# A mixture-of-experts layer on one core: packed chunks of rows, and the experts' weights loaded and split for each chunk

## The chip, the cores and the metric

One core of a Trainium2 chip runs the whole layer. The metric is the device time of one execution in microseconds, lower is better.

## What is computed

The input holds 32 x 512 tokens of 256 numbers, all in float32. Cut to what matters:

```python
x = layernorm(x + attention(x))          # 16 heads of 16, 512 keys
logits = x @ Wg.T                        # 8 experts
top_v, top_i = top_k(logits, 2); gates = softmax(top_v)
# each expert takes its first cap = 16384*2*1.25/8 = 5120 rows, the rest are dropped
h = rows_of_expert @ W1[e]               # 256 -> 1024
h = gelu(h[:, :512]) * h[:, 512:]
y = h @ W2[e]                            # 512 -> 256
x = layernorm(x + sum over both experts of gate * y)
```

## The kernel before

The kernel has three stages with a barrier between them. `attention` goes through the 32 sequences and computes attention, the first layer norm and the routing. Its GpSimd queue scatters every token's row (256 numbers and four more: token, gate data, expert) into the DRAM table `expert_rows`, at the next free slot of its expert. The table has 8 x 5120 rows, that is ten chunks of 512 rows per expert, filled with blanks early on. `experts` works through all 80 chunks of this table, expert by expert. `final_norm` computes the last layer norm.

In `experts` a chunk takes this way. SyncE (SP) loads its rows (L1032, four loads of 128 KB, and L1033, the four extra numbers). VectorE (DVE) transposes them (L1178). ScalarE (ACT) rounds them to the matmul's type as a high part (L1129), and VectorE makes the low part, the remainder (L1184). TensorE (PE) multiplies high by high, low by high and high by low, six matmuls of 512 columns for each of eight results (L1091, `hidden`). ScalarE computes gelu (L1133), VectorE the product (L1190), ScalarE its high part (L1139), VectorE its low part (L1195). TensorE makes the output (L1104, `output`), ScalarE scales it by the gate (L1147), and GpSimd (POOL) adds it into DRAM with four indirect adds (L1061). VectorE's `meta` works out gate and token number of the chunk (L1207 to L1211), and SP may load the rows of chunk n+2 only after it. The loops on all engines run in step by semaphores; `output` of chunk n-1 stands between `hidden` 1 and 2 of chunk n.

The weights of an expert are split in high and low parts as well. They are double-buffered by expert: in the second chunk of each expert SP loads the next expert's weights (L175, L176), and GpSimd makes both parts after its adds (L1074, L1076):

```python
for i, (raw, hi, lo) in enumerate(weights.pieces(1 - k.par)):
    pool.tensor_copy(hi, raw).then_inc(s_whi, 1)
    pool.wait_ge(s_whi, k.e * W_PIECES + (i + 1))
    pool.tensor_tensor(lo, raw, hi.bitcast(F32), ALU.subtract).then_inc(s_w, 1)
```

The three pieces are two halves of W1 and the whole of W2, each 128 x 1024 numbers. Most chunks run in hardware loops (`engine.Fori`). The weights of expert 0 are loaded at the end of `attention`, and split there by ScalarE (L660) and VectorE (L920).

## Time and profile before

| | |
|---|---|
| median of 3 runs | 3536.07 us (3529.52 to 3536.82) |
| profiled execution, its own time | 3539.23 us |
| its span | 3537.5 us |
| PE busy | 3328.4 us (94%) |
| DVE busy | 2489.7 us (70%) |
| ACT busy | 2001.0 us (57%) |
| POOL busy | 1156.9 us (33%) |
| mean granted clock of TensorE | 0.968 |

The profile is of one execution. Busy shares are averages over three stages with different limits: `attention` lasts until about 2046 us, `experts` until about 3430 us, `final_norm` until the end. Names such as `out<-ps_out,gate` are the program's tiles, written from read. An engine's idle time is given in brackets with what ended it.

### The profile page before, as it was taken

What the parts mean: (1) busy time and instruction counts of PE and PEld (TensorE: products, weight loads), DVE (VectorE), ACT (ScalarE), POOL (GpSimd) and SP (SyncE); (2) the same over time, 40 slices, a digit from 0 to 9 for tenths busy, and PEclk for the clock granted to TensorE, in tenths of its full rate; (3) what the DMA queues carried; (4) which work ended last, traced back from release to release, by engine and by line L of the source; (5) the groups of instructions that cost most, each with busy time, mean ns of one, the idle gap of its engine ahead of it and who ended that gap; (6) DMA issues with size and microseconds to landing.
All of it is one profiled execution on the core that took longest, in us unless ns stands there. A gap on an engine that the chain in (4) does not pass through costs nothing. (4 is left out here: it accounts for less than half of the span.)

```text
span 3537.5 us, 60085 instructions
## 1 busy us (share of the span) xinstructions
PE 3328.4 (94%) x19714; PEld 2116.9 (60%) x19714; DVE 2489.7 (70%) x5865; ACT 2001.0 (57%) x3877; POOL 1156.9 (33%) x925
## 2 busy tenths in 40 slices
PE   6999999999999999999999779999999999999960
PEld 3444444444444444444444368888888888888850
DVE  5888888888888888888888445545554545554439
ACT  2777777777777777777777434444444444444420
POOL 1013232222313131313222243435343435343334
PEclk7999999999999999999999789999999999999985
DMA  3444555333323232333333244444344434442439
GB/s 98 146 152 153 162 157 166 107 96 86 97 79 101 78 100 79 100 83 88 91 83 93 61 80 63 74 65 69 54 72 61 79 61 63 66 62 45 62 68 339
DMA packets 397856, 339.51 MB, mean 96 GB/s; under 512 B 257720, under 2 KB 315456, under 8 KB 397632
## 3 DMA queue, kind: packets, MB, share of 16 engines
q1 hardware_dynamic: 334656, 252.20, 27.3%
q0 software_dynamic: 58368, 67.74, 11.3%
q10 hardware_dynamic: 4608, 16.78, 1.2%
q8 instruction: 117, 1.92, 0.2%
q14 instruction: 107, 0.88, 0.1%
HBM read 89.92 MB, written 152.17 MB: 68 GB/s over the span
## 5 line engine op out<-in xcount | busy, mean ns | idle before, releaser
L882 DVE TENSOR_REDUCE peak<-ps_rows 128x1 f32<-128x512 f32 x2048 | 1340.2, 679 | 284.1 <-PE ps_rows L557 280.2
L648 ACT ACTIVATE probs<-ps_cols 128x512 f32<-128x512 f32 x2048 | 1118.5, 599 | 266.7 <-PE ps_cols L567 254.8
L1091 PE MATMUL ps_hid<-x_hi,stack 128*128 128x512 f32 x2560 | 805.0, 396 | 32.3 <-DVE x_lo L1184 27.8
L567 PE MATMUL ps_cols<-stack 50*128 50x512 f32 x2048 | 797.9, 460 | 6.0 <-ACT probs L648 5.8
L557 PE MATMUL ps_rows<-stack 48*128 48x512 f32 x2048 | 763.4, 450 | 9.9 <-DMA stack<-qk_lo 7.7
L1061 POOL DMA_INDIRECT x<-out,token x320 | 503.8, 1574 | 800.2 <-ACT out L1147 641.4
L1190 DVE TENSOR_TENSOR hid<-ps_hid,act_in 128x512 f32<-128x512 f32 x320 | 218.9, 688 | 597.6 <-ACT act_in L1133 597.3
L1091 PEld LDWEIGHTS ps_hid<-x_hi,stack 128*128 128x128 f32 x2560 | 476.9, 189 | 142.0 <-DVE x_lo L1184 27.9
L580 PE MATMUL ps_pv<-probs,v 128*17 128x512 f32 x4096 | 541.6, 601 | 1.2 <-ACT probs L648 1.2
L557 PEld LDWEIGHTS ps_rows<-stack 48*128 48x128 f32 x2048 | 314.5, 187 | 372.8 <-DVE peak L882 264.5
L1091 PE MATMUL ps_hid<-x_lo,stack 128*128 128x512 f32 x1280 | 505.8, 395 | 0.0
L422 POOL TENSOR_SCALAR var_eps<-mv 128x4 f32<-128x4 f32 x32 | 7.5, 233 | 1415.1 <-DVE mv L752 1415.1
L1104 PE MATMUL ps_out<-w_buf,h_hi 128*128 128x256 f32 x2560 | 464.8, 283 | 2.9 <-DVE h_lo L1195 2.9
L1104 PEld LDWEIGHTS ps_out<-w_buf,h_hi 128*128 128x128 f32 x2560 | 402.7, 190 | 10.1 <-issue 3.3
L1133 ACT ACTIVATE act_in<-ps_hid 128x512 f32<-128x512 f32 x320 | 190.0, 596 | 309.4 <-PE ps_hid L1091 309.4
L1104 PE MATMUL ps_out<-w_buf,h_lo 128*128 128x256 f32 x1280 | 363.6, 284 | 0.0
L567 PEld LDWEIGHTS ps_cols<-stack 50*128 50x128 f32 x2048 | 322.0, 185 | 60.6 <-ACT probs L648 44.4
L447 POOL DMA_INDIRECT expert_rows<-row,slot x256 | 254.4, 994 | 85.6 <-issue 81.9
L1147 ACT ACTIVATE out<-ps_out,gate 128x256 f32<-128x256 f32 x320 | 125.4, 475 | 273.6 <-PE ps_out L1104 273.6
L1091 PEld LDWEIGHTS ps_hid<-x_lo,stack 128*128 128x128 f32 x1280 | 241.4, 189 | 57.0
L1195 DVE TENSOR_TENSOR h_lo<-hid,h_hi 128x512 fp32r<-128x512 f32 x320 | 237.3, 746 | 15.3 <-ACT h_hi L1139 0.4
L1104 PEld LDWEIGHTS ps_out<-w_buf,h_lo 128*128 128x128 f32 x1280 | 242.4, 189 | 0.0
(131 smaller groups left out, 3603.2 us busy)
## 6 DMA issues: line engine op xcount, KB each, us to landing
stack<-qk_hi SPq DMA_DIRECT2D x1024, 64.0 KB, 2.3
expert_rows<-blank SPq DMA_DIRECT2D x80, 520.0 KB, 3.9
quarters<-expert_rows SPq DMA_DIRECT2D x320, 128.0 KB, 2.7
stack<-qk_lo SPq DMA_DIRECT2D x512, 64.0 KB, 2.3
xs<-in_L_attn_x SPq DMA_DIRECT2D x32, 512.0 KB, 3.7
x<-row SPq DMA_DIRECT2D x32, 512.0 KB
fy<-x SPq DMA_DIRECT2D x32, 512.0 KB, 4.6
out<-fz ACTq DMA_DIRECT2D x32, 512.0 KB, 4.8
```

The source lines that it names most:

```text
L447: pool.indirect_dma_start(table, bass.IndirectOffsetOnAxis(ap=slot[:, c:c + 1], axis=0), row[it.odd][:, t, :], None, bounds_check=table.sh ...
L557: pe.matmul(ps_rows[n % ROWS][:], q_stack[s][part, h, t * P:(t + 1) * P], k_stack[s][part, h, :], start=True, stop=True).then_inc(s_rows, 1)
L567: pe.matmul(ps_cols[j % 2][:], k_stack[g][part, h, t * P:(t + 1) * P], q_stack[g][part, h, :], start=True, stop=True).then_inc(s_cols, 1)
L580: last = pe.matmul(ps_pv[32 * h:32 * h + HD + 1, :], v[par][:, t, HG * g + h, :], probs[:, (HG * t + h) % RING, :], start=t == 0, stop=t = ...
L648: act.activation(probs[:, j % RING, :], ps_cols[j % 2][:], ACT.Exp, scale=SCALE).then_inc(s_exp, 1)
L882: dve.tensor_reduce(peak[s % 2][:, u:u + 1], ps_rows[n % ROWS][:], AX.X, ALU.max, negate=True).then_inc(s_max, 1)
L1061: pool.indirect_dma_start(x1_dram, bass.IndirectOffsetOnAxis(ap=token[buf][:, t:t + 1], axis=0), out[buf][:, t, :], None, bounds_check=n_t ...
L1091: last = pe.matmul(ps_hid[f % 2][:, part, :], w[c.par][k][:, cols], xx[c.odd][:, k, :], start=i == 0, stop=i == 3 * KT - 1)
L1104: last = pe.matmul(ps_out[:, t, :], hh[buf][:, f, t * P:(t + 1) * P], w[par][:, f, :], start=i == 0, stop=i == 3 * FT - 1)
L1133: act.activation(act_in[f % 2][:], ps_hid[f % 2][:, 0, :], ACT.Gelu).then_inc(s_gelu, 1)
L1190: dve.tensor_tensor(hid[f % 2][:], ps_hid[f % 2][:, 1, :], act_in[f % 2][:], ALU.mult).then_inc(s_mul, 1)
L1195: dve.tensor_tensor(h_lo[c.odd][:, f, :], hid[f % 2][:], h_hi[c.odd][:, f, :].bitcast(F32), ALU.subtract).then_inc(s_hlo, 1)
```

## The change

The change makes the number of chunks 72. At the end of `attention` VectorE reads the experts' totals (TensorE adds the counts over the partitions), caps them at 5120, counts each expert's chunks and writes for each of 72 places the chunk of the table and the number of the expert. At most 71 chunks can hold rows, since 64 full chunks hold all rows and each expert but one can add a partly filled one. Places beyond the last used chunk read an extra blank chunk at the table's end.

Since the expert of a place is known only on the chip, the weights are loaded for every chunk, by a number that SP reads from SBUF (`value_load`), into the raw buffers, and split every time: the high parts on ScalarE (`high_w`), the remainders on GpSimd (`low_w`). The two buffers of split weights alternate by chunk. The loop over the chunks is written out in full on every engine. `gate_part` compares with the plan's expert number instead of a counter.

```diff
+    def load_w1(self, engine, e, s_raw1):
         for a in range(QUARTERS):
-            engine.dma_start(self.raw1[a * BLOCK:(a + 1) * BLOCK], self.w1_rows[e, a]).then_inc(s_raw, 16)
-        engine.dma_start(self.raw2, self.w2_rows[e]).then_inc(s_raw, 16)
+            engine.dma_start(self.raw1[a * BLOCK:(a + 1) * BLOCK], self.w1_rows[e, a]).then_inc(s_raw1, 16)
+    def load_w2(self, engine, e, s_raw2):
+        engine.dma_start(self.raw2, self.w2_rows[e]).then_inc(s_raw2, 16)
...
+        self.per = cap // SEQ
+        self.n_chunks = -(-(n_tokens * TOPK // SEQ + EXPERTS - 1) // 2) * 2
+        self.numbers = sb("plan_numbers", [P, 2, self.n_chunks], U32)
+        self.expert = sb("plan_expert", [P, self.n_chunks])
+    def rows(self, engine, n):
+        return engine.value_load(self.numbers[0:1, 0, n:n + 1], min_val=0, max_val=EXPERTS * self.per)
+    def weights(self, engine, n):
+        return engine.value_load(self.numbers[0:1, 1, n:n + 1], min_val=0, max_val=EXPERTS - 1)
...
+            pe.wait_ge(s_pvout, n_seq * GROUPS)
+            pe.wait_ge(s_route, (n_seq - 1) * ROUTE + COUNTED + 3)
+            pe.matmul(ps_pv[:, 0:EXPERTS], ones[:], carry[:], start=True, stop=True).then_inc(s_total, 1)
...
+            numbers = chunk_no[:].rearrange("p (c a) -> p c a", a=1).to_broadcast([P, plan.n_chunks, EXPERTS])
+            dve.wait_ge(s_total, 1)
+            dve.tensor_scalar(total[:], ps_pv[:, 0:EXPERTS], float(cap), None, ALU.min).then_inc(s_plan, 1)
+            dve.wait_ge(s_plan, 3)
+            dve.tensor_scalar(total[:, 0:1], total[:, 0:1], SEQ + 1.0, None, ALU.max).then_inc(s_plan, 1)
+            dve.wait_ge(s_plan, 4)
+            dve.tensor_tensor(reached[:], total[:].rearrange("p (e a) -> p e a", a=1).to_broadcast([P, EXPERTS, per]),
+                              steps[:].rearrange("p (a i) -> p a i", a=1).to_broadcast([P, EXPERTS, per]),
+                              ALU.is_gt).then_inc(s_plan, 1)
+            dve.wait_ge(s_plan, 5)
+            dve.tensor_reduce(own_chunks[:], reached[:], AX.X, ALU.add).then_inc(s_plan, 1)
+            dve.wait_ge(s_plan, 6)
+            for e in range(EXPERTS):
+                dve.tensor_copy(upto[:, e, 0:e + 1], own_chunks[:, 0:e + 1]).then_inc(s_plan, 1)
+            dve.wait_ge(s_plan, 6 + EXPERTS)
+            dve.tensor_reduce(ends[:], upto[:], AX.X, ALU.add).then_inc(s_plan, 1)
+            dve.wait_ge(s_plan, 7 + EXPERTS)
+            dve.tensor_tensor(ended[:], by_chunk(ends), numbers, ALU.is_le).then_inc(s_plan, 1)
+            dve.wait_ge(s_plan, 8 + EXPERTS)
+            dve.tensor_reduce(plan.expert[:], ended[:], AX.X, ALU.add).then_inc(s_plan, 1)
+            dve.tensor_tensor(ended_at[:], ended[:], by_chunk(ends), ALU.mult).then_inc(s_plan, 1)
+            dve.wait_ge(s_plan, 10 + EXPERTS)
+            dve.tensor_scalar(plan.numbers[:, 1], plan.expert[:], float(EXPERTS - 1), None, ALU.min).then_inc(s_plan, 1)
+            dve.tensor_reduce(start[:], ended_at[:], AX.X, ALU.max).then_inc(s_plan, 1)
+            dve.scalar_tensor_tensor(place[:], plan.expert[:], float(per), chunk_no[:], ALU.mult, ALU.add).then_inc(s_plan, 1)
+            dve.wait_ge(s_plan, 13 + EXPERTS)
+            dve.tensor_tensor(place[:], place[:], start[:], ALU.subtract).then_inc(s_plan, 1)
+            dve.wait_ge(s_plan, 14 + EXPERTS)
+            dve.tensor_scalar(plan.numbers[:, 0], place[:], float(EXPERTS * per), None, ALU.min).then_inc(s_plan, 1)
...
+            load_rows(0)
+            load_rows(1)
+            for n in range(n_chunks):
+                if n + 1 < n_chunks:
+                    expert = 0 if n == 0 else plan.weights(sp, n + 1)
+                    wait(sp, s_w, n * W_PIECES - 1)
+                    weights.load_w1(sp, expert, s_raw1)
+                    wait(sp, s_w, n * W_PIECES)
+                    weights.load_w2(sp, expert, s_raw2)
+                if n + 2 < n_chunks:
+                    sp.wait_ge(s_turn, n * KT + KT)
+                    sp.wait_ge(s_meta, n + 1)
+                    load_rows(n + 2)
...
+            def low_w(n, i):
+                raw, hi, lo = weights.pieces(n % 2)[i]
+                pool.wait_ge(s_whi, (n - 1) * W_PIECES + (i + 1))
+                pool.tensor_tensor(lo, raw, hi.bitcast(F32), ALU.subtract).then_inc(s_w, 1)
+            for n in range(n_chunks):
+                if n + 1 < n_chunks:
+                    low_w(n + 1, 0)
+                    low_w(n + 1, 1)
+                if n:
+                    add_out(n - 1)
+                if n + 1 < n_chunks:
+                    low_w(n + 1, 2)
+            add_out(n_chunks - 1)
...
+                wait(pe, s_w, n * W_PIECES - 1)
+                pe.wait_ge(s_xlo, n * KT + KT)
+                hidden(n, 0)
+                hidden(n, 1)
+                if n:
+                    output(n - 1)
+                hidden(n, 2)
+                hidden(n, 3)
...
+            def high_w(n, i):
+                raw, hi, _ = weights.pieces(n % 2)[i]
+                if i == 0:
+                    act.wait_ge(s_raw1, n * W1_LOADED)
+                elif i == 2:
+                    act.wait_ge(s_raw2, n * W2_LOADED)
+                act.copy(hi, raw).then_inc(s_whi, 1)
...
+                more = n + 1 < n_chunks
+                if more:
+                    high_x(n + 1)
+                gelu(n, 0)
+                if more:
+                    high_w(n + 1, 0)
+                gelu(n, 1)
+                high_h(n, 0)
+                if more:
+                    high_w(n + 1, 1)
+                high_h(n, 1)
+                if n:
+                    scale(n - 1)
+                if more:
+                    high_w(n + 1, 2)
+                gelu(n, 2)
+                gelu(n, 3)
+                high_h(n, 2)
+                high_h(n, 3)
```

How the rows of instructions move. First SP, in a chunk late in `experts`; `quarters` and `meta_rows` are the rows of a chunk, `probs` is the raw buffer of the weights, `plan_numbers` the plan. Before, at the last switch of expert:

```order
L1032 DMA quarters<-expert_rows 32x16x64 [waits s_turn,s_meta]
L1032 DMA quarters<-expert_rows 32x16x64 x3
L1033 DMA meta_rows<-expert_rows 128x4x4
L175 DMA probs<-in_L_ffn_W 32x2x1024 [waits s_w]
L175 DMA probs<-in_L_ffn_W 32x2x1024 x3
L176 DMA probs<-in_L_ffn_W 128x4x256
L1032 DMA quarters<-expert_rows 32x16x64 [waits s_turn,s_meta]
```

Now, in every chunk, the loads of rows between the two register reads and those of weights behind them:

```order
L201 TENSOR_LOAD plan_numbers [waits s_meta,s_turn]
L201 ISA x2
L1078 ISA
L1078 DMA quarters<-expert_rows 32x16x64
...
L1079 ISA
L1079 DMA meta_rows<-expert_rows 128x4x4
L204 TENSOR_LOAD plan_numbers
L204 ISA x2
L176 ISA [waits s_w]
L176 DMA probs<-in_L_ffn_W 32x2x1024
...
L179 ISA [waits s_w]
L179 DMA probs<-in_L_ffn_W 128x4x256
```

The pairs of ISA and DMA stand four times for `quarters` and for the first `probs`. Two reads of registers have come in, the five loads of weights now come in every chunk, and the weights of the next chunk wait in the queue behind the rows of the same chunk.

Second GpSimd, before at a switch of expert (`x` is the sum in DRAM, `stack` and `w_buf` the split weights):

```order
L1061 DMA x<-out,token 16384x256 [waits s_scaled,s_add]
L1061 DMA x<-out,token 16384x256 x3
L1074 CAST stack<-probs 128x1024 [waits s_raw,s_out]
L1076 TENSOR_TENSOR stack<-probs,stack 128x1024 [waits s_whi]
L1074 CAST stack<-probs 128x1024
L1076 TENSOR_TENSOR stack<-probs,stack 128x1024 [waits s_whi]
L1074 CAST w_buf<-probs 128x1024
L1076 TENSOR_TENSOR w_buf<-probs,w_buf 128x1024 [waits s_whi]
```

and now in every chunk:

```order
L1110 TENSOR_TENSOR stack<-probs,stack 128x1024 [waits s_whi] x2
L1103 DMA x<-out,token 16384x256 [waits s_add,s_scaled]
L1103 DMA x<-out,token 16384x256 x3
L1110 TENSOR_TENSOR w_buf<-probs,w_buf 128x1024 [waits s_whi]
L1110 TENSOR_TENSOR stack<-probs,stack 128x1024 [waits s_whi] x2
```

The casts have left GpSimd, and two of the three subtractions stand ahead of the adds. The casts are now on ScalarE, in every chunk:

```order
L1168 CAST x_hi<-turned 128x512 [waits s_turn] x2
L1180 ACTIVATE act_in<-ps_hid 128x512 [waits s_hid]
L1176 CAST stack<-probs 128x1024 [waits s_raw1]
L1180 ACTIVATE act_in<-ps_hid 128x512 [waits s_hid]
L1186 CAST h_hi<-hid 128x512 [waits s_mul,s_out]
L1176 CAST stack<-probs 128x1024
L1186 CAST h_hi<-hid 128x512 [waits s_mul]
L1194 ACTIVATE out<-ps_out,gate 128x256 [waits s_add,s_meta,s_out]
L1194 ACTIVATE out<-ps_out,gate 128x256 x3
L1176 CAST w_buf<-probs 128x1024 [waits s_raw2]
L1180 ACTIVATE act_in<-ps_hid 128x512 [waits s_hid] x2
L1186 CAST h_hi<-hid 128x512 [waits s_mul] x2
```

The three casts of weights (L1176) stand between gelus and high parts of h, each in front of instructions that VectorE's products and low parts wait for.

## Rows read from the trace of the kernel before

**Rows 1.** Timeline, GpSimd: start us, us, engine line op, names, count [idle before].
```profile
2082.07 1.58 POOL L1061 DMA_INDIRECT x<-out,token  x1 [39.80 <-ACT out L1147]
...
2234.74 1.55 POOL L1061 DMA_INDIRECT x<-out,token  x1 [9.61 <-ACT out L1147]
...
2240.30 1.67 POOL L1061 DMA_INDIRECT x<-out,token  x1 [0.30 <-issue]
...
2251.62 1.55 POOL L1061 DMA_INDIRECT x<-out,token  x1 [9.65 <-ACT out L1147]
...
3406.42 1.56 POOL L1061 DMA_INDIRECT x<-out,token  x1 [9.59 <-ACT out L1147]
```

**Rows 2.** Waits from 2150 to 3390 us: engine, name, line, releaser: us, times, longest.
```profile
PE ps_hid L1091 <- DVE hid L1190: 4.2, 6, 1.4
```

**Rows 3.** Timeline, ScalarE, a chunk without a switch.
```profile
2243.91 0.61 ACT L1139 CAST h_hi<-hid 128x512 fp32r<-128x512 f32 x1
...
2249.17 1.57 ACT L1147 ACTIVATE out<-ps_out,gate 128x256 f32<-128x256 f32 x4 [3.78 <-PE ps_out L1104]
...
2251.97 0.60 ACT L1133 ACTIVATE act_in<-ps_hid 128x512 f32<-128x512 f32 x1 [1.23 <-PE ps_hid L1091]
```

**Rows 4.** Timeline, VectorE, the same chunk.
```profile
2241.86 1.29 DVE L1184 TENSOR_TENSOR x_lo<-turned,x_hi 128x512 fp32r<-128x512 f32 x2
...
2244.65 1.46 DVE L1195 TENSOR_TENSOR h_lo<-hid,h_hi 128x512 fp32r<-128x512 f32 x2
...
2246.37 0.17 DVE L1211 COPY token<-meta_rows 128x4 uint32<-128x4 uint32 x1
```

**Rows 5.** Timeline, the DMA issues of SyncE, around the first switch shown.
```profile
2233.74 1.72 SPq L175 DMA_DIRECT2D probs<-in_L_ffn_W  x4
...
2235.50 0.43 SPq L176 DMA_DIRECT2D probs<-in_L_ffn_W  x1
...
2246.62 1.91 SPq L1032 DMA_DIRECT2D quarters<-expert_rows  x4
...
2248.57 0.49 SPq L1033 DMA_DIRECT2D meta_rows<-expert_rows  x1
```

**Rows 6.** Landing of the loads of line 175, then 176, 2225 to 2245 us.
```profile
DMA to landing us min/median/max: 3.4/4.5/5.7
...
DMA to landing us min/median/max: 6.5/6.5/6.5
```

**Rows 7.** Timeline, GpSimd and then VectorE, a chunk with a split of weights.
```profile
2260.03 2.73 POOL L1076 TENSOR_TENSOR stack<-probs,stack 128x1024 fp32r<-128x1024 f32 x1
...
2264.29 2.40 POOL L1076 TENSOR_TENSOR stack<-probs,stack 128x1024 fp32r<-128x1024 f32 x1
...
2268.22 2.73 POOL L1076 TENSOR_TENSOR w_buf<-probs,w_buf 128x1024 fp32r<-128x1024 f32 x1
...
2258.78 4.53 DVE L1184 TENSOR_TENSOR x_lo<-turned,x_hi 128x512 fp32r<-128x512 f32 x2
...
2264.95 3.74 DVE L1195 TENSOR_TENSOR h_lo<-hid,h_hi 128x512 fp32r<-128x512 f32 x2 [0.44 <-ACT h_hi L1139]
...
2268.61 2.36 DVE L1207 SCALAR_TENSOR_TENSOR gate_part<-meta_rows,expert_no 128x4 f32<-128x4 f32 x1
```

**Rows 8.** Timeline, ScalarE and VectorE, end of the first stage.
```profile
2028.42 1.04 ACT L660 CAST w_buf<-probs 128x1024 fp32r<-128x1024 f32 x1
...
2032.54 1.22 DVE L920 TENSOR_TENSOR w_buf<-probs,w_buf 128x1024 fp32r<-128x1024 f32 x1
...
2046.79 0.06 DVE L1171 MEMSET expert_no<- 128x1 f32 x1 [13.02 <-PEq L197]
```

**Rows 9.** Busy by stretch: us; PE, PEld, DVE, ACT, POOL; PEclk, DMA share, GB/s.
```profile
1984.00:1988.00 4.00, 3.23 (x22) 0.83 (x14) 0.43 (x3) 3.18 (x7) 0.00 (x0) 1.00 0.00 0
...
2056.00:2060.00 4.00, 4.00 (x11) 3.08 (x10) 1.29 (x2) 1.87 (x3) 0.00 (x0) 0.53 0.00 0
...
2060.00:2064.00 4.00, 4.00 (x19) 3.24 (x18) 1.31 (x3) 1.67 (x3) 0.00 (x0) 1.00 0.01 4
```

More of the change, by code:

```diff
@@ L151 @@
 QUARTERS, BLOCK = P // 32, 32
-LOADED = 16 * (QUARTERS + 1)
+ROWS_LOADED = 16 * (QUARTERS + 1)
+W1_LOADED, W2_LOADED = 16 * QUARTERS, 16
 W_PIECES = 3
@@ L273, in attention @@
         token = sb("token", [P, TILES])
+        total = sb("total", [P, EXPERTS])
+        steps = sb("steps", [P, per])
+        reached = sb("reached", [P, EXPERTS, per])
+        own_chunks = sb("own_chunks", [P, EXPERTS])
+        upto = sb("upto", [P, EXPERTS, EXPERTS])
+        ends = sb("ends", [P, EXPERTS])
+        chunk_no = sb("chunk_no", [P, plan.n_chunks])
+        ended = sb("ended", [P, plan.n_chunks, EXPERTS])
+        ended_at = sb("ended_at", [P, plan.n_chunks, EXPERTS])
+        start = sb("start", [P, plan.n_chunks])
+        place = sb("place", [P, plan.n_chunks])
         s_const = sem("s_const")
@@ L370, in body @@
                         sp.wait_ge(s_pv, n_seq * UNITS)
-                        weights.load(sp, 0, s_raw)
+                        weights.load_w1(sp, 0, s_raw1)
+                        weights.load_w2(sp, 0, s_raw2)
                     if it.filling:
@@ L1107, in output @@
                 last.then_inc(s_out, 1)
-            def body(k):
-                if k.lead and not k.odd:
-                    wait(pe, s_w, k.e * W_PIECES)
-                pe.wait_ge(s_xlo, k.n * KT + KT)
-                hidden(k, 0)
-                hidden(k, 1)
-                if not k.first:
-                    output(1 - k.par if k.lead and not k.odd else k.par, 1 - k.odd, k.n - 1)
-                hidden(k, 2)
-                hidden(k, 3)
-            chunks(pe, body)
-            output(1, (n_chunks - 1) % 2, n_chunks - 1)
+            for n in range(n_chunks):
+                wait(pe, s_w, n * W_PIECES - 1)
[6 more added lines that the diff above has]
+                hidden(n, 3)
@@ L1213, in _ @@
-            turn(0, 0, LOADED)
-            low_x(0, 0)
-            def body(k):
-                if not (k.last and k.odd):
-                    turn(1 - k.odd, k.n + 1, (k.half + (k.odd + 1)) * LOADED)
-                    low_x(1 - k.odd, k.n + 1)
-                product(k, 0)
-                product(k, 1)
-                low_h(k, 0)
-                low_h(k, 1)
-                meta(k)
-                product(k, 2)
-                product(k, 3)
-                low_h(k, 2)
-                low_h(k, 3)
@@ L1230, in _, with meta @@
-            chunks(dve, body)
+            def meta(n):
+                wait(dve, s_scaled, n * TILES - TILES)
+                wait(dve, s_add, n * ADDED - ADDED)
+                r = meta_rows[n % 2]
+                dve.scalar_tensor_tensor(gate_part[:], r[:, :, C_E0 - DIM], plan.expert[:, n:n + 1], r[:, :, C_DIFF - DIM],
+                                         ALU.is_equal, ALU.mult).then_inc(s_gp, 1)
+                dve.wait_ge(s_gp, n + 1)
+                dve.tensor_tensor(gate[n % 2][:], gate_part[:], r[:, :, C_G1 - DIM], ALU.add)
+                dve.tensor_copy(token[n % 2][:], r[:].bitcast(U32)[:, :, C_ID - DIM]).then_inc(s_meta, 1)
@@ L1233, in final_norm @@
+            turn(0)
+            low_x(0)
+            for n in range(n_chunks):
+                if n + 1 < n_chunks:
+                    turn(n + 1)
+                    low_x(n + 1)
+                product(n, 0)
+                product(n, 1)
+                low_h(n, 0)
+                low_h(n, 1)
+                meta(n)
+                product(n, 2)
+                product(n, 3)
+                low_h(n, 2)
+                low_h(n, 3)
 def final_norm(nc, y_dram, out_dram):
```

202 lines of the change are left out of this document (69 added, 133 removed).

## The prediction

> **What bounds the kernel now.** The kernel has three stages, and the change touches the second, so I read that one. The GpSimd adds mark its rhythm: every chunk of 512 rows ends in four indirect adds, and the first of chunk 0 starts at 2082.07 us, the first of chunk 78 at 3406.42 us [rows 1]. That is 1324.35 us for 78 chunks, 16.98 us each. A chunk without a switch of expert takes 16.88 us (2251.62 - 2234.74), [rows 1] as well. The waits of the stage say who sets this: TensorE waited 4.2 us in 1240 us, six times, always for the product on VectorE [rows 2]. So TensorE bounds the stage, and the only disturbance is the seven switches of expert. Every other engine has slack: ScalarE's scaling of a chunk starts at 2249.17 us and its next gelu at 2251.97 us [rows 3], and GpSimd's adds fill only 7.2 us of a chunk (2234.74 to 2241.97 us) [rows 1].
>
> **What is taken away.** 80 chunks become 72. TensorE's work in a chunk is the same, whatever the rows hold. If a chunk kept its length, 8 x 16.98 = 136 us would go.
>
> **What is added to every chunk.** Before, weights were loaded and split seven times in the stage; now 71 times. Five loads are issued on SP, three casts of 128x1024 are made on ScalarE, three subtractions of 128x1024 on GpSimd, and SP reads two numbers from SBUF into registers. I cost each.
>
> *ScalarE* gets 3 x 1.04 us (the same cast at the end of the first stage) [rows 8]. Two stand between gelu 0 and the scaling, where no matmul of the chunk is short of them. The third stands between scaling (ends 2250.74) and gelu (starts 2251.97): 1.23 us of slack takes 1.04. By itself this costs nothing.
>
> *GpSimd* gets 3 x 2.40 to 2.73 us [rows 7]; with 7.2 us of adds and a 0.9 us handover from ScalarE this is about 16 us of a chunk of 16.88. It fits, barely, and is no bound alone.
>
> *VectorE* gets no instruction, but its subtractions are held up. Undisturbed, two low parts of x take 1.29 us and two of the hidden rows 1.46 us [rows 4]. While GpSimd splits weights, the same pairs take 4.53 and 3.74 us, and a gate product of 128x4 takes 2.36 us, ending just when GpSimd's subtraction does (2270.97 against 2270.95) [rows 7]. So a VectorE instruction with two SBUF inputs waits for the whole GpSimd instruction. The products that read PSUM are not held.
>
> *SP and the loads* close a circle, and this is where I think the new bound lies. SP's queue is in order: the rows of chunk n+2 (after meta of chunk n), then the first-layer weights of n+2, then the second-layer ones. ScalarE can cast those weights only when they have landed, GpSimd subtracts only then, VectorE's low parts wait for GpSimd, meta stands behind them, and meta releases the next rows. One turn, from meta to meta:
>
> 1. meta ends at 2246.54 us (2246.37 + 0.17) [rows 4], SP issues at 2246.62 [rows 5]: 0.08.
> 2. Register read for the rows: no row shows one. Below, 0.17, the shortest VectorE copy [rows 4]; above, a whole DMA on this queue, which for these loads is 3.4 us at least [rows 6]. I take 0.75, a DMA issue on SP (0.49) and a handover between engines with it (about 0.25), because it moves one word and no packets. The Trainium skill, DMA: Bandwidth & Descriptors, section "Latency and other measured facts", gives a floor of about 0.6 us for a tensor_load; by that each turn would be 0.3 us shorter than by mine, 21 us over the stage. No trace here shows it.
> 3. Issue of five row loads: 2246.62 to 2249.06: 2.44 [rows 5].
> 4. Second register read: 0.75.
> 5. First-layer weights. The four issues start at 2233.74 and take 1.72 [rows 5]; the latest landed up to 5.7 us after its own issue, so about 1.4 + 5.7 = 7.1 after the first [rows 6]. The second-layer load (0.5 MB, behind it then) will now come later. It landed at 2235.50 + 6.5 = 2242.0, and the 1.5 MB took some 6.2 us, so its share in front of the last quarter was about 0.9. I take 6.2; the bounds are 4.8 (1.4 + the shortest landing, 3.4) and 7.1.
> 6. From landing to meta: handover 0.1, cast 1.04, GpSimd's first subtraction 2.40, one low part on VectorE 0.73, GpSimd's second 2.40, the other low part 0.73, then gate, sum and token 0.43 (2246.54 less 2244.65 less 1.46): 7.8 [rows 4, 7, 8]. If VectorE went first each time, only ScalarE's chain would count: two casts, a gelu, two h casts at 0.6 [rows 3], a low part and 0.43, some 5.1. With 2.73 for both subtractions it is 8.5.
>
> Sum: 0.08 + 0.75 + 2.44 + 0.75 + 6.2 + 7.8 = **18.0 us**. That is longer than 16.88, so TensorE should wait about 1.1 us per chunk, for the product behind meta. The lower bound of the circle (12.7) lies below TensorE's 16.88, which is then the period. The upper (0.08 + 3.4 + 2.44 + 3.4 + 7.1 + 8.5) is 24.9.
>
> *The second-layer weights* have a circle of their own through adds (7.2), the last subtraction (2.7), the load (6.5 at most), cast, gelu, product and TensorE's 11.3 us to the next scaling: about 33 us for two chunks, 16.5 each. No bound, but close.
>
> *The plan* is some 22 small VectorE instructions of about 0.2 us and four of 576 elements (under 1 us each): 8 us at most. VectorE ends its last subtraction at 2033.76 us and idles 13 us to the stage's start at 2046.79, because GpSimd's scatters are still going [rows 8]. Cost nothing; without that cover 8 us. One more blank fill on SP, two counters at the start and the longer straight-line program: nothing, for SP and GpSimd idle there; both signs within 3 us.
>
> **The sum.** Counting 70 steps between first adds of chunk 0 and 70 in place of 78: time = 3539.2 - 1324.4 + 70 x T, with T the new period. The profiled run was 3539.2 us, 3.2 above the median, so against the median I use 3536 - 1324.4 + 70 x T. With T = 18.0: 2211.6 + 1260 = **3472 us**. The change loses its gain at T = 18.92. A measurement here can tell about 0.2%, 7 us, or 0.1 us of T.
>
> **Rivals.**
> *A, the circle does not close.* Loads land early enough, or VectorE's low parts mostly slip in front of GpSimd. T = 16.9, 3394 us. For it: all three lower bounds lie well below mine. Against it: GpSimd would have to lose a race that it won in rows 7. Chance 0.20.
> *Forecast*, T from 17.0 to 18.9, 3402 to 3535 us. Chance 0.50.
> *C, slower: the register reads are dear.* They stand in front of both groups of loads, on the queue that everything waits for. The point from which this decides is 1.2 us each (0.92 more in the turn). At 1.5 us each T = 19.5 and the time is 3577 us; at the price of a whole DMA (3.4) T = 23.3, 3843 us. For it: nothing hides them. Against it: one word is not a DMA. Chance 0.22.
> *D, slower: the clock.* TensorE was granted 1.00 (2.4 GHz) in a stretch where it was busy 3.23 of 4 us, and 0.5 (1.2 GHz) in the idle start of the stage, where 11 matmuls took the time of 19 [rows 9]. If waits of 1 us in each chunk brought the low clock, each chunk would take 16.9 x 19/11 = 29 us: 4242 us if always, about 3680 if a fifth of the chunks. Busy at 94% is well above the 81% at which the row still shows full clock. The Trainium skill, TensorE: Matmul & The Clock Gate, section "HAM oscillation — how this bites in real kernels", warns that pauses between bursts of matmuls bring this on; by it the slow case would be real, by the row it is not. Chance 0.08.
> That the chunks are not fewer is excluded: the loops are written out for 72.
>
> **How the numbers follow.** The point is the likeliest case, 3472. Its own range is 3402 to 3535. The range of 8 in 10 goes down to A (3390) and up to C at 1.5 us (3577), and leaves out dearer reads and D. Faster: A and nearly all of the forecast, 0.70; same 0.05; slower, C and most of D, 0.25.
>
> **What would show it.** Right: chunks 17.5 to 18.5 us apart by the adds; TensorE waiting about 1 us per chunk for the product; ScalarE waiting several us for the weights in front of its first cast; VectorE's low parts of h near 2.4 us each; SP taking 4 us from meta to the first weight load. Step 2 is wrong if the gap in front of the row loads is not near 0.75; step 5 if the weights land in under 5 or over 7 us; step 6 if landing to meta is not 7 to 8.5. The forecast as a whole is wrong if ScalarE does not wait for raw weights, or if the clock in the stage is under 1.00.

## The result, and the profile after

| | before | after |
|---|---|---|
| median of 4 runs | 3532.80 us (3528.88 to 3536.82) | 3596.55 us (3593.22 to 3601.08) |
| profiled execution, its own time | 3539.23 us | 3595.22 us |
| its span | 3537.5 us | 3593.7 us |
| mean granted clock of TensorE | 0.968 | 0.957 |

The change makes the kernel **slower**: the ratio is 1.0185, 95% interval 1.0168 to 1.0202, clear of the noise (on another chip it was 1.0223, below). Forecast was 3472 us, faster, with a range up to 3577.

The page's busy times and two of its 40-slice rows, kernel after:

```profile
PE 3245.0 (90%) x18947; PEld 2014.0 (56%) x18947; DVE 2632.9 (73%) x5758; ACT 2123.3 (59%) x3978; POOL 1608.1 (45%) x1066
...
PEclk7999999999999999999999699999999999999985
DMA  3445454333333333333332366666666666666639
```

From slice 23 on the second stage runs: the DMA engines are busy for six tenths there, where the first stage has three. GpSimd has 450 us more work than before, VectorE 143, ScalarE 122.

The rhythm, GpSimd's timeline, first adds of chunk 0 and of chunk 70 (as [rows 1]):

```profile
2085.36 1.86 POOL L1103 DMA_INDIRECT x<-out,token  x1 [0.16 <-issue]
...
3465.41 1.56 POOL L1103 DMA_INDIRECT x<-out,token  x1 [5.02 <-ACT out L1194]
```

These are 1380.05 us for 70 steps, a period T of 19.71 us instead of 16.98. The part of the time outside these steps is 3595.22 - 1380.05 = 2215.2 us; before it was 3539.23 - 1324.35 = 2214.9. So the whole loss is in T.

Waits of the kernel after, 2200 to 3400 us (as [rows 2]: engine, name, line, releaser: us in total, times, longest):

```profile
ACT x_hi L1168 <- DVE turned L1227: 390.8, 60, 7.8
DVE turned L1227 <- DMA meta_rows<-expert_rows: 301.9, 60, 6.3
POOL stack L1110 <- ACT stack L1176: 250.2, 60, 5.9
DVE hid L1239 <- ACT act_in L1180: 165.2, 63, 4.4
ACT stack L1176 <- DMA probs<-in_L_ffn_W: 141.9, 60, 3.8
PE ps_hid L1132 <- DVE hid L1239: 122.9, 73, 2.7
```

and of SP, the engine that issues the loads:

```profile
SPq L1092 <- DVE token L1256: 593.4, 61, 11.4
```

In each of 60 chunks every engine waits for another one, and the list closes on itself: SP waits for VectorE's token (the end of `meta`), VectorE for the rows that SP loads, ScalarE for the weights that SP loads behind them, GpSimd for ScalarE. TensorE, which before waited 4.2 us in the stage [rows 2], waits 123 us in 1200.

**One turn of the circle**, from the end of one `meta` to the end of the next. VectorE, SP, ScalarE, GpSimd, VectorE from the timelines of 2700 to 2745 us (start us, us, engine, line):

```profile
2718.29 0.16 DVE L1256 COPY token<-meta_rows 128x4 uint32<-128x4 uint32 x1
...
2719.25 2.04 SPq L1078 DMA_DIRECT2D quarters<-expert_rows  x4
2721.48 0.39 SPq L1079 DMA_DIRECT2D meta_rows<-expert_rows  x1
2722.62 1.81 SPq L176 DMA_DIRECT2D probs<-in_L_ffn_W  x4
...
2725.81 1.30 DVE L1227 STREAM_TRANSPOSE turned<-quarters 128x512 f32<-128x512 f32 x2 [4.79 <-DMA meta_rows<-expert_rows]
...
2728.16 0.39 SPq L179 DMA_DIRECT2D probs<-in_L_ffn_W  x1
...
2730.41 1.05 ACT L1176 CAST stack<-probs 128x1024 fp32r<-128x1024 f32 x1 [2.15 <-DMA probs<-in_L_ffn_W]
...
2731.54 5.23 POOL L1110 TENSOR_TENSOR stack<-probs,stack 128x1024 fp32r<-128x1024 f32 x2 [3.54 <-ACT stack L1176]
...
2732.60 4.72 DVE L1244 TENSOR_TENSOR h_lo<-hid,h_hi 128x512 fp32r<-128x512 f32 x2
...
2737.58 0.16 DVE L1256 COPY token<-meta_rows 128x4 uint32<-128x4 uint32 x1
```

Token ends at 2718.45; 0.80 us later the rows are issued, for 2.62 us; after 0.75 us more the first weight load is issued; 7.79 us later ScalarE casts; 7.33 us after that the next token ends (2737.74): 19.29 us. The same five differences, taken over the 68 turns from 2100 to 3440 us in which the trace names the weights' landing as what ScalarE's cast waited for:

| step | forecast | measured, mean |
|---|---|---|
| 1 + 2: meta to first row load | 0.83 | 0.82 |
| 3: issue of five row loads | 2.44 | 2.85 |
| 4: to the first weight load | 0.75 | 0.84 |
| 5: first weight load issued, to ScalarE's cast | 6.3 | 7.95 |
| 6: from the cast's start to meta | 7.7 | 7.32 |
| turn | 18.0 | 19.77 |

(The forecast's handover of 0.1 us between landing and cast stands in row 5 here.)

TensorE in this turn, its timeline and then one-microsecond stretches (us; PE, PEld, DVE, ACT, POOL busy; granted clock, DMA share, GB/s):

```profile
2719.19 1.19 PE L1132 MATMUL ps_hid<-x_hi,stack 128*128 128x512 f32 x2 [2.54 <-DVE hid L1239]
```

```profile
2719.00:2720.00 1.00, 0.81 (x2) 0.75 (x3) 0.91 (x3) 0.93 (x2) 0.69 (x2) 0.50 0.00 0
2720.00:2721.00 1.00, 1.00 (x3) 0.75 (x3) 1.00 (x2) 0.29 (x1) 1.00 (x1) 0.50 1.03 97
...
2724.00:2725.00 1.00, 1.00 (x6) 0.82 (x5) 0.00 (x0) 0.00 (x0) 0.99 (x2) 1.00 1.51 267
...
2730.00:2731.00 1.00, 1.00 (x11) 1.00 (x10) 0.00 (x0) 0.59 (x1) 0.00 (x0) 1.00 0.94 301
2731.00:2732.00 1.00, 1.00 (x10) 1.00 (x10) 0.01 (x1) 1.00 (x3) 0.46 (x1) 1.00 0.52 183
```

TensorE stands still for 2.54 us, then has a granted clock of 0.50 (1.2 GHz) until about 2722 us: the matmul pair of 0.63 us takes 1.19. And the DMA engines are full, or nearly, from 2720 to 2731 us, which covers the whole time in which the circle waits for them. (The profile gives shares over 1 there; I read them as full.)

### The profile page after: what moved, and what is told of

Its sections match the earlier page's. It is cut to its first block and busy times, and to the rows that moved or that the text cites. A ratio compares the mean times of both kernels' runs of the same rounds, so it can differ in the third digit from the quotient of the medians.

```text
span 3593.7 us, 57839 instructions
## 1 busy us (share of the span) xinstructions
PE 3245.0 (90%) x18947; PEld 2014.0 (56%) x18947; DVE 2632.9 (73%) x5758; ACT 2123.3 (59%) x3978; POOL 1608.1 (45%) x1066
## 5 line engine op out<-in xcount | busy, mean ns | idle before, releaser
L1132 PE MATMUL ps_hid<-x_hi,stack 128*128 128x512 f32 x2304 | 768.4, 416 | 170.8 <-DVE hid L1239 143.1
L1132 PEld LDWEIGHTS ps_hid<-x_hi,stack 128*128 128x128 f32 x2304 | 444.3, 199 | 305.2 <-issue 162.1
L1110 POOL TENSOR_TENSOR stack<-probs,stack 128x1024 fp32r<-128x1024 f32 x142 | 370.0, 2631 | 315.6 <-ACT stack L1176 315.6
L1132 PE MATMUL ps_hid<-x_lo,stack 128*128 128x512 f32 x1152 | 473.1, 411 | 0.0
L1244 DVE TENSOR_TENSOR h_lo<-hid,h_hi 128x512 fp32r<-128x512 f32 x288 | 430.8, 1533 | 6.7 <-ACT h_hi L1186 0.7
L1146 PE MATMUL ps_out<-w_buf,h_hi 128*128 128x256 f32 x2304 | 407.0, 280 | 2.9 <-DVE h_lo L1244 2.9
L1168 ACT CAST x_hi<-turned 128x512 fp32r<-128x512 f32 x144 | 87.4, 622 | 479.9 <-DVE turned L1227 479.9
L1146 PEld LDWEIGHTS ps_out<-w_buf,h_hi 128*128 128x128 f32 x2304 | 356.4, 188 | 9.7 <-issue 3.3
L1227 DVE STREAM_TRANSPOSE turned<-quarters 128x512 f32<-128x512 f32 x144 | 94.0, 690 | 364.1 <-DMA meta_rows<-expert_rows 364.1
L1146 PE MATMUL ps_out<-w_buf,h_lo 128*128 128x256 f32 x1152 | 321.9, 279 | 0.0
```

What stands on the lines that cost most here:

```text
L1132: last = pe.matmul(ps_hid[f % 2][:, part, :], w[n % 2][k][:, cols], xx[n % 2][:, k, :], start=i == 0, stop=i == 3 * KT - 1)
L1146: last = pe.matmul(ps_out[:, t, :], hh[n % 2][:, f, t * P:(t + 1) * P], w[n % 2][:, f, :], start=i == 0, stop=i == 3 * FT - 1)
L1244: dve.tensor_tensor(h_lo[n % 2][:, f, :], hid[f % 2][:], h_hi[n % 2][:, f, :].bitcast(F32), ALU.subtract).then_inc(s_hlo, 1)
```

## The experiments

The theory and its rivals. **Circle**: the turn above sets the period; whatever shortens it shortens T by as much, until TensorE's own 16.9 us or the next longest circle. **Volume**: the weight traffic itself (1.5 MB a chunk) is what the stage can't carry. **Lock**: GpSimd's subtractions hold VectorE up, and that alone makes the chunk long. **Clock**: the half-clock phases of TensorE make it long. Ratios are against the kernel before on the same chip. T is the mean distance of the tokens of all chunks in the profiled execution; after has 19.64 by this count, before 16.90. Steps of a turn are given as in the table above.

**e_reads: the two register reads taken out of the turn.** SP reads both numbers before it waits.

```diff
-                    expert = 0 if n == 0 else plan.weights(sp, n + 1)
...
                 if n + 2 < n_chunks:
+                    rows = plan.rows(sp, n + 2)
+                    expert = plan.weights(sp, n + 2)
                     sp.wait_ge(s_turn, n * KT + KT)
                     sp.wait_ge(s_meta, n + 1)
-                    load_rows(n + 2)
+                    load_rows(n + 2, rows)
```

> Both register reads of chunk n+2 are made before SP waits for meta of chunk n, so they leave the circle. Circle theory: a turn of 19.6 us loses 0.74 + 0.84 = 1.6 us, so T = 18.1 and the time is 3597 - 70 x 1.6 = about 3487 us, and the gap from the end of meta to the first row load falls from 0.8 to 0.1 us. Lock theory (VectorE and GpSimd holding each other up set the rhythm by themselves): no change, 3597. Load-volume theory (the DMA engines can't move the 2.5 MB of a chunk faster): no change, 3597.

Measured: 3519.42 us, ratio 0.9961 (0.9945 to 0.9977), T 18.58. The gain is 77 us, two thirds of what the circle had promised; the other two theories expected none. The same place on VectorE and SP, timelines of 2700 to 2740 us:

```profile
2716.68 0.17 DVE L1257 COPY token<-meta_rows 128x4 uint32<-128x4 uint32 x1
...
2717.06 2.08 SPq L1077 DMA_DIRECT2D quarters<-expert_rows  x4
2719.33 0.39 SPq L1078 DMA_DIRECT2D meta_rows<-expert_rows  x1
2719.90 2.16 SPq L176 DMA_DIRECT2D probs<-in_L_ffn_W  x4
```

Over 64 turns the steps are 0.22, 2.75, 0.20, 8.20, 7.35, in sum 18.71. Each read is worth 0.60 and 0.64 us. The Trainium skill, DMA: Bandwidth & Descriptors, section "Latency and other measured facts", gives a floor of some 600 ns for a tensor_load; these two differences agree with it. What the expectation took out, 0.74 and 0.84, held handovers that stayed. The landing of the weights, which now stand closer behind the rows, is 0.25 us longer than in after. Chips differ by nearly as much (r_after, below); e_dvereads has this on one chip and shows that the term is not a constant.

**e_halfw1: half of the first-layer weights loaded.** Columns 0 to 511 of W1 only; this kernel leaves the rest of the weights out.

```diff
-            engine.dma_start(self.raw1[a * BLOCK:(a + 1) * BLOCK], self.w1_rows[e, a]).then_inc(s_raw1, 16)
+            engine.dma_start(self.raw1[a * BLOCK:(a + 1) * BLOCK, :, 0:FF], self.w1_rows[e, a][:, :, 0:FF]).then_inc(s_raw1, 16)
```

> Only half the columns of the first-layer weights are loaded (the other half keeps old values), so part of the computation is left out; instructions and waits are the same. Circle theory: the landing term of 7.95 us falls by about 2.3 us (0.5 MB at 220 GB/s), T = 17.3, time about 3435 us. Load-volume theory: the bytes of a chunk fall by a fifth, T = 15.7, so TensorE's 16.9 sets it, 3405. Lock theory: no change, 3597.

Measured: 3440.21 us, ratio 0.9743 (0.9727 to 0.9759), T 17.45. The landing fell from 7.95 to 5.55 us, the others stayed (0.81, 3.00, 0.95, 7.43), in the 31 turns in which ScalarE still waited for it. In these turns half of a megabyte is worth 2.4 us; T fell by 2.2. Waits, 2200 to 3200 us:

```profile
DVE turned L1227 <- DMA meta_rows<-expert_rows: 235.7, 56, 5.8
ACT stack L1176 <- DMA probs<-in_L_ffn_W: 16.9, 29, 1.6
```

In 57 chunks VectorE waits for its rows 56 times, ScalarE for the weights only 29 times: in the other turns something else closes the circle. There is a second way round from meta to meta, through the rows of the chunk. In the turn of after shown above it takes 0.80 us to the first row load, 6.56 to the transposes (2725.81 us) and 11.93 to the next token, and the last part holds the 2.15 us in which ScalarE waited for the weights. Without that wait it would be some 17.1 us, an estimate from these rows, and T came out at 17.45. Circle and volume both say that T falls, so this run only prices the term; the next run tells them apart.

**e_meta: the circle opened.** SP waits for `meta` only because it would overwrite `meta_rows`. With four buffers it need not; the wait on the transposes stays.

```diff
-        meta_rows = [sb(f"meta_rows{i}", [P, TILES, ROW - DIM]) for i in range(2)]
+        meta_rows = [sb(f"meta_rows{i}", [P, TILES, ROW - DIM]) for i in range(4)]
...
-                sp.dma_start(meta_rows[n % 2][:], chunk_meta[rows]).then_inc(s_rows[n % 2], 16)
+                sp.dma_start(meta_rows[n % 4][:], chunk_meta[rows]).then_inc(s_rows[n % 2], 16)
...
                     sp.wait_ge(s_turn, n * KT + KT)
-                    sp.wait_ge(s_meta, n + 1)
                     load_rows(n + 2)
```

> Four buffers for the extra numbers in place of two, and SP no longer waits for meta before it loads the rows of chunk n+2; the bytes, the splits and the reads stay. Circle theory: the circle is open, the first-layer weights wait only for GpSimd's second subtraction; its own circle is 0.1 + 7 + 6.4 = 14 us, so TensorE's 16.9 sets the period: 3400 to 3425 us. Lock theory: no change, 3597. Load-volume theory: no change, 3597.

Measured: 3403.62 us, ratio 0.9639 (0.9623 to 0.9655), T 16.91. Waits of TensorE for the product, 2150 to 3200 us, and SP's and VectorE's timeline from 2700 us:

```profile
PE ps_hid L1131 <- DVE hid L1238: 4.1, 2, 2.4
```

```profile
2716.59 0.39 SPq L179 DMA_DIRECT2D probs<-in_L_ffn_W  x1
2717.75 2.59 SPq L1078 DMA_DIRECT2D quarters<-expert_rows  x4
...
2721.77 1.81 SPq L176 DMA_DIRECT2D probs<-in_L_ffn_W  x4
...
2722.56 0.16 DVE L1255 COPY token<-meta_rows 128x4 uint32<-128x4 uint32 x1
```

The rows now go out right behind the second-layer weights, 4.8 us ahead of the token that they used to wait for. The same bytes are moved, the same splits made by the same engines, and T is that of the kernel before (16.90). So neither the volume nor the lock was what held T at 19.6; one wait was, for a buffer of 8 KB. It makes the circle a shown cause: all of the 2.7 us per chunk that after had lost against before went with that wait, which stood in front of the rows and so in both ways round. The clock rose again with it, so this run doesn't price the clock; see rival D below. A run with four buffers and the wait kept was not made.

**e_dve: the remainders on VectorE.** The three subtractions of a chunk move from GpSimd to VectorE, between products and low parts; the wait stays.

```diff
                 product(n, 0)
+                low_w(n + 1, 0)
                 product(n, 1)
                 low_h(n, 0)
+                low_w(n + 1, 1)
                 low_h(n, 1)
...
                 product(n, 2)
+                low_w(n + 1, 2)
                 product(n, 3)
```

> VectorE makes the three remainders of the weights (1.22 us each) in place of GpSimd; GpSimd only adds. Circle theory: from cast to meta the turn falls from 7.3 to about 5.8 us, nothing else: T = 18.1, about 3490 us. Lock theory: no lock is left, T = 16.9, 3405 us. Load-volume theory: no change, 3597.

Measured: 3462.63 us, ratio 0.9808 (0.9792 to 0.9825), T 17.84. VectorE's timeline from 2700 us:

```profile
2722.03 1.23 DVE L1253 TENSOR_TENSOR stack<-probs,stack 128x1024 fp32r<-128x1024 f32 x1 [3.10 <-ACT stack L1166]
...
2724.37 1.22 DVE L1253 TENSOR_TENSOR stack<-probs,stack 128x1024 fp32r<-128x1024 f32 x1
2725.51 0.69 DVE L1234 TENSOR_TENSOR h_lo<-hid,h_hi 128x512 fp32r<-128x512 f32 x1
2726.45 0.17 DVE L1246 COPY token<-meta_rows 128x4 uint32<-128x4 uint32 x1
```

A weight's remainder takes 1.22 us instead of 2.4 to 2.7, a low part of h 0.69 instead of 2.4 (4.72 for two above). Step 6 fell from 7.32 to 5.66 us, the turn to 17.98 (66 turns), near the 18.1 that the circle theory said; with the lock as the whole cause it would have been 16.9. So the lock is real, but as a term of the circle, worth 1.66 us.

*The following batch (e_order to e_metadve) ran on a chip whose first stage took about 225 us longer, with and without the change (before: 3758.18 us); only its ratios and its second stage are compared. The changed kernel itself was not run there, so its steps are compared with those of another chip; between two other chips its T differed by 0.22 us (r_after, below).*

**e_order: the weights ahead of the rows.** SP issues the first-layer weights of chunk n+2 before the rows of n+2, hence outside the wait for `meta`.

The old loads of chunk n+1 at this place are gone, and those of chunk 1 stand ahead of the loop.

```diff
...
                 if n + 2 < n_chunks:
+                    expert = plan.weights(sp, n + 2)
+                    sp.wait_ge(s_w, (n + 1) * W_PIECES - 1)
+                    weights.load_w1(sp, expert, s_raw1)
                     sp.wait_ge(s_turn, n * KT + KT)
                     sp.wait_ge(s_meta, n + 1)
                     load_rows(n + 2)
+                    sp.wait_ge(s_w, (n + 1) * W_PIECES)
+                    weights.load_w2(sp, expert, s_raw2)
```

> SP issues the first-layer weights of chunk n+2 ahead of the rows of chunk n+2, as soon as GpSimd's second subtraction is done; the wait for meta stays in front of the rows. Theory that the weights' landing of 7.95 us is long because the rows are just in front of them: landing falls to about 6, and the circle through the weights is open; what is left runs meta, read 0.8, issue 2.8, landing of rows 5, transposes, low parts and products back to meta, 15 to 17.8 us: T = 16.9 to 17.8, 3400 to 3465 us. Theory that the adds alone make it long: landing stays near 8, but T still falls since the circle is shorter.

Measured: 3824.61 us, ratio 1.0182 (1.0163 to 1.0201), T 19.65. My expectation missed: as slow as the changed kernel instead of 2 to 4% under before. SP's and VectorE's timelines of 2900 to 2945 us, and the wait that ends VectorE's longest idle time, 2400 to 3400 us:

```profile
2905.49 1.84 SPq L176 DMA_DIRECT2D probs<-in_L_ffn_W  x4
2908.15 2.02 SPq L1078 DMA_DIRECT2D quarters<-expert_rows  x4
...
2906.11 0.16 DVE L1257 COPY token<-meta_rows 128x4 uint32<-128x4 uint32 x1
2915.96 1.31 DVE L1228 STREAM_TRANSPOSE turned<-quarters 128x512 f32<-128x512 f32 x2 [6.34 <-DMA meta_rows<-expert_rows]
```

```profile
DVE turned L1228 <- DMA meta_rows<-expert_rows: 367.5, 51, 8.7
```

The weights are no longer waited for; the rows are. They stand 0.8 us behind 1 MB of weights, and the transposes start 7.8 us after their first issue (8.06 in the mean of 73 turns; 6.82 in after, 68 turns). SP was also still busy issuing the weights when meta ended, so the first row load goes out 1.88 us after meta (2906.27 to 2908.15) instead of 0.8. Behind the rows come the transposes, the high and low parts of x and the hidden layer, 9.67 us to the next token at 2925.63 us: 1.88 + 7.81 + 9.67 = 19.36. The circle was closed again by the way through the rows, at about the same length. I had taken 5 us for the rows' landing, from the kernel in which no weights stood in front of them, and left out that SP is busy. The order within one in-order queue decides who pays for the transfers, not whether they are paid.

**e_noadd: the adds move no data.** The bound of the indirect adds is 0, so that they skip nearly all rows.

```diff
-                        bounds_check=n_tokens - 1, oob_is_err=False, compute_op=ALU.add).then_inc(s_add, 16)
+                        bounds_check=0, oob_is_err=False, compute_op=ALU.add).then_inc(s_add, 16)
```

> The changed kernel with adds whose row numbers are nearly all out of bounds: GpSimd still makes them, but they move no data, so the sums are left out. If the adds' traffic is what makes the first-layer weights land late (7.95 us after their first issue, 6.2 forecast), landing falls to 6.5 or less, T to 18.2, 3500 us or less. If it isn't, landing and time stay, 3597 us.

Measured: 3750.96 us, ratio 0.9977 (0.9961 to 0.9994), T 18.68; steps 0.81, 2.70, 0.79, 7.19, 7.32 (60 turns). The result lies between the two cases of the expectation. Against after the landing is shorter by 0.76 us of 7.95, so the adds' traffic is worth about that, give or take the 0.2 us by which chips differ. Of the excess of 1.65 us over the forecast some 0.9 stays without the adds; this kernel doesn't say whose it is.

**e_meta80: e_meta with 80 chunks.** `self.n_chunks = 80` besides.

> The version without SP's wait for meta, with 80 chunks in place of 72 (the last ones blank). If TensorE sets the period of 16.9 us there, 8 chunks cost 8 x 16.9 = 135 us: 3404 + 135 = 3539 us, the time of the kernel before. If something else than the chunk count made that version fast, the difference is not 135.

Measured: 3773.69 us, ratio 1.0044 (1.0027 to 1.0060), T 17.02: with 80 chunks, all with weights of their own, the kernel is 15.5 us slower than before. What the count alone is worth is read against the next run, on the same chip.

**e_metadve: e_meta and the remainders on VectorE.** Both edits above.

> The version without SP's wait for meta, with the weights' remainders on VectorE, so that GpSimd and VectorE never hold each other up. Circle theory: TensorE is the bound already, T stays 16.9, 3395 to 3405 us. If the lock still cost something there, the time falls by more than 10 us.

Measured: 3618.12 us, ratio 0.9624 (0.9608 to 0.9640), T 16.80. Whether the lock still cost something in e_meta, run on another chip (0.9639), this run alone doesn't tell; the last batch does. It lies 155.6 us under e_meta80. The remainders' place is 19.3 us of that, if it is worth here what it is on another chip (r_meta less r_metadve, below); that leaves 136 us for 8 chunks, and 8 x 16.9 is 135. So the packing is worth about what its count says once TensorE bounds the chunk. That e_meta gains 127 us over before and not 136 fits with e_meta80, which with as many chunks as before is 15.5 us slower than it; I take this for the price of the chunks' own weights, but no run separates it from the rest of the change.

**The last batch**, on a chip like the first (before: 3531.31 us, 9 runs), five rounds each, to have the changed kernel and the best ones side by side.

> The changed kernel once more, so that it stands beside the next three on one chip. Ratio to the kernel before 1.0185 as at first, if the result does not hang on the chip.

> The version without SP's wait for meta once more, beside the others on one chip: ratio 0.964 to the kernel before.

> Without SP's wait for meta and with the remainders on VectorE, on the same chip as the version that has them on GpSimd. In the first traces TensorE was busy 500 of 500 us here and 473 to 497 of 500 there. If that was the lock, this is 10 to 15 us faster, ratio 0.960; if TensorE sets both, the same.

| kernel | us | ratio (95%) |
|---|---|---|
| r_after | 3610.88 | 1.0223 (1.0209 to 1.0237) |
| r_meta | 3405.40 | 0.9642 (0.9629 to 0.9655) |
| r_metadve | 3386.12 | 0.9598 (0.9585 to 0.9611) |

r_meta came out as expected. r_after did not: 1.0223 lies outside the first interval, while the kernel before takes the same time on both chips. The loss is in T again, 19.86 instead of 19.64, with a landing of 8.17 us instead of 7.95 (67 turns), so the size of the loss hangs a little on the chip; why was not tried. r_metadve gained more than the 10 to 15 us expected.

Busy by stretch of 2200 to 3200 us; before, after (the first profile), r_meta, r_metadve in this order:

```profile
2200.00:3200.00 1000.00, 995.80 (x5650) 868.30 (x5649) 531.63 (x891) 431.35 (x823) 442.57 (x272) 1.00 0.43 66
```

```profile
2200.00:3200.00 1000.00, 894.97 (x4829) 755.92 (x4828) 596.59 (x759) 499.08 (x861) 733.18 (x354) 0.96 0.65 131
```

```profile
2200.00:3200.00 1000.00, 993.58 (x5616) 857.92 (x5615) 834.24 (x881) 586.37 (x997) 810.01 (x412) 1.00 0.82 153
```

```profile
2200.00:3200.00 1000.00, 1000.00 (x5711) 870.24 (x5710) 682.11 (x1070) 594.30 (x1011) 441.87 (x237) 1.00 0.80 155
```

The DMA engines carry more in r_meta (0.82) than in after (0.65), and TensorE is busy again, at full clock. In r_meta VectorE is "busy" 834 us, of which a good part must be standing behind GpSimd; with the remainders moved over to it, it is busy 682 us, *less*, though it does more. That last edit gives 19.3 us, 0.27 a chunk (T 17.00 and 16.75), so in r_meta the lock still cost something: TensorE was busy 993.58 of 1000 us there and all of them here. r_metadve is the best version found and beats both kernels: 4.0% under before, 6.2% under after.

**e_dvereads: two terms taken out, the wait kept.** The edits of e_dve and e_reads together.

> SP's wait for meta stays; the register reads are made early and VectorE makes the remainders. If the terms of the circle add up, it takes 19.77 - 1.24 (reads) - 1.66 (cast to meta) = 16.9 us, TensorE's own 16.9, and this version comes near the one with the open circle: ratio 0.96 to 0.97. If each edit alone only moved the same slack, it stays at the better of the two, 0.981.

Measured: 3420.92 us, ratio 0.9691 (0.9678 to 0.9704), T 17.24; steps 0.22, 2.57, 0.19, 8.70, 5.66, in sum 17.35 (67 turns). The reads and step 6 add up as single edits had them; only the landing takes back a part (8.17 in r_after on the same chip, now 8.70). With 17.35 the circle is still longer than TensorE's chunk, and TensorE still waits 23 us for the product from 2200 to 3200 us: shortening every stage of the circle gets less than cutting it in one place.

## Why the prediction was wrong

It was wrong in sign, by 124.5 us. Its mechanism, the circle from meta to meta, was right, and **one term of the sum was mis-sized**: step 5, the landing of the first-layer weights, 6.2 us forecast and 7.85 measured.

- *The form of the sum* held: outside the 70 steps 2215.2 us where 2214.8 was taken. By its own profiled execution the forecast is 2214.8 + 1260 = 3474.8; 3595.22 was measured, 120.4 more, and 70 x (19.71 - 18.0) = 120. The other 4 us are the medians' distance from their profiled executions.
- *Steps 1, 2 and 4*, the register reads: forecast 0.75 each, handover included; measured 0.74 and 0.84, of which e_reads shows 0.60 and 0.64 to be the read. Right.
- *Step 3*, the issue of five row loads: 2.44 forecast, 2.85 measured. Too low by 0.4, about what step 6 was too high by; that these two cancel is luck. Why an issue takes longer here was not tried.
- *Step 5*: 6.2 forecast, bounds 4.8 to 7.1; measured 7.85 from first issue to landing, if the handover is 0.1. **This step failed, with its upper bound.** 70 x 1.65 = 116 us, the whole miss but for the small terms. By the prediction's own sign (weights landing in over 7 us) it is wrong. I took the landings of one switch, the one in [rows 5, 6], subtracted 0.9 us for the second-layer load behind it, and called the unshortened value the upper bound. The trace of before has seven such switches, all with rows issued just ahead, and the longest landing in them is 6.5, 5.7, 5.8, 5.4, 6.0, 5.1 and 5.9 us, in order of time. Line 175 around the first switch (2060 to 2085 us), kernel before, then line 176 in one turn (2722 to 2725 us), kernel after:

```profile
DMA to landing us min/median/max: 4.1/5.1/6.5
```

```profile
DMA to landing us min/median/max: 4.2/5.2/6.3
```

  The worst switch of before looks like an ordinary turn of after. By the same working it gives 1.4 + 6.5 = 7.9 us, the measured value; with it the sum is 19.7 and the time 3591 us. So the upper bound had to be 7.9, not 7.1: one sample is no bound. And the subtraction of 0.9 had no row of its own: in after the second-layer load is issued some 4 us later than in before (2728.16 us in the turn above), and the first-layer ones land no earlier.
- *Step 6*, landing to meta: 7.8 forecast, 7.4 measured, handover included, inside the bounds of 5.1 to 8.5 and inside its own sign of 7 to 8.5. That GpSimd would win the race for the port was right in nearly every turn (e_dve: 5.66 without it).
- *The other signs*: TensorE waits 2.0 us a chunk for the product (122.9 us in 61 chunks), where about 1 was named; SP takes 4.5 us from meta to the first weight load, where 4 was named; ScalarE waits 2.4 us for the weights, where several were named. Two signs fail outright: the chunks are 19.7 us apart and not 17.5 to 18.5, and the clock in the stage is 0.96, where under 1.00 was to mean that the forecast as a whole is wrong. That last sign was badly chosen, as rival D shows.
- *What hides what*: the casts on ScalarE and GpSimd's 16 us a chunk made no bound, as said (e_meta has T 16.91 with both). The prediction overlooked the second way round, through the rows: with the weights' wait gone it would still be near 17.1 us (e_halfw1, e_order). VectorE's plan lies from 2030.61 to 2036.24 us, 5.6 us, and VectorE then still idles before the stage:

```profile
2030.61 0.16 DVE L976 TENSOR_SCALAR total<-ps_pv 128x8 f32<-128x8 f32 x1
...
2036.04 0.20 DVE L1002 TENSOR_SCALAR plan_numbers<-place 128x72 uint32<-128x72 f32 x1
...
2049.11 1.30 DVE L1227 STREAM_TRANSPOSE turned<-quarters 128x512 f32<-128x512 f32 x2 [12.87 <-DMA meta_rows<-expert_rows]
```

  So it cost nothing, as predicted.
- *Rival A* (the circle does not close, T 16.9, 3394 us) did not come, but its number did once the wait was cut: 3403.6 us.
- *Rival C* (dear register reads, 3577 us) has nearly the time that came, by luck, and not its cause: the reads cost 0.6 us each.
- *Rival D* (clock): the granted clock of the stage fell to 0.96, with 0.50 after the stall of 2.54 us shown above. So the row of 1.00 at 3.23 busy us of 4 was no safe ground: this stage shows the low clock all the same. Nor does the length of the stall decide it by itself. Two stalls of 2.64 us each, ending at 2996.30 and at 3016.00 us, and the stretches behind them:

```profile
2996.50:2997.50 1.00, 1.00 (x5) 0.81 (x5) 0.91 (x3) 0.91 (x2) 0.70 (x2) 1.00 0.44 34
3016.20:3017.20 1.00, 1.00 (x3) 0.81 (x4) 0.91 (x3) 0.90 (x2) 0.70 (x2) 0.50 0.54 26
```

  The Trainium skill, TensorE: Matmul & The Clock Gate, section "HAM oscillation — how this bites in real kernels", warns of waits between bursts of matmuls; its own case has longer waits than the 1 us forecast here, so by itself it did not make the slow case real. The rows of 2719 to 2721 us agree with the warning, and the row of 2996.50 us shows that it doesn't always come true. The low clock cost nothing that shows: of the turns of after from 2100 to 3440 us, the 29 with a mean granted clock under 0.95 take 19.75 us and the 39 at full clock 19.79 (r_after: 28 with 20.00, 39 with 20.04). It fits with the steps, which lie on VectorE, SP, a transfer, ScalarE and GpSimd and add up to T without TensorE. No run was made that holds the clock alone. The price that the prediction gave for low clock in a fifth of the chunks, 3680 us, does not follow from its own terms either: a fifth at 29 and the rest at 18.0 us give T = 20.2 and 3626 us.
- *The chances*: break-even lay at T = 18.92, 0.9 us above the forecast, while step 5 alone had a room of 0.9 upward by its own bounds. A chance of 0.25 for slower was too small for a sum of six terms that all had to hold within that.

Still open is what in the landing makes the 7.95 us: e_noadd gives some 0.8 to the adds, e_halfw1 2.4 to half of the weights; how the rest divides between rows and weights was not tried, nor why six of the seven switches of before had it shorter.

## What to carry to other kernels

When a change puts a load behind a wait in an in-order queue, follow the wait back to that load: if the chain closes, add up its turn, and see first whether more buffers of a small tile cut it, since that was worth 2.7 us a chunk here and shortening its stages one by one 1.0 to 2.2. Look for the second longest way round as well: it is what is left when one load is made cheaper or moved. Take a transfer's duration from every place where the trace has it, and the longest as the bound. And where break-even lies within one term's uncertainty, say so in the chances.

## What the runs showed of the hardware that was not expected

- **A load's landing grew as the rest of the turn shrank.** On one chip the first-layer weights were cast 8.17 us after their first issue where the rest of the turn took 11.9 us, and 8.70 where it took 8.7 (r_after, e_dvereads). The runs e_reads and e_dve (8.20 and 8.10, rest 10.5 and 9.9) lie above after (7.95, rest 11.8) as well, by about as much as chips differ. Time saved ahead of this transfer, on DMA engines that were full, was given back in part; by what mechanism was not tried.
- **VectorE's wait behind GpSimd counts as busy.** It was busy 834 us per 1000 in r_meta and 682 in r_metadve, with three more instructions of 1.22 us in each chunk. The Trainium skill, SBUF — State Buffer, section "Who interferes with whom", describes the port pair that both share as an exclusive lock; the low part of h agrees, 0.69 us alone and 2.4 beside GpSimd's subtraction.
- **GpSimd's subtraction of 128x1024 takes about twice VectorE's time**: 2.6 against 1.22 us (after, e_dve).
- **The same stall can be followed by either clock.** After a stall of 2.54 us the granted clock stood at 0.50 for some 3 us; of two stalls of 2.64 us one was followed by 1.00 and one by 0.50. None of this lengthened a turn (19.75 us with, 19.79 without).
